# A fused attention and FP4 feed-forward block: one AV copy on ScalarE, division 22 steps behind, and reordered projections, transposes and last divisions

## The reference

```python
def reference(x, Wq, bq, Wk, bk, Wv, bv, Wo, bo, alpha, w_gate, w_up, w_down):   # x: (8, 2048, 1024)
    x = _layernorm(x + attn(x))          # over the last axis, eps 1e-5
    x = _layernorm(x + ffn(x))
    return x

def attn(x):                             # 16 heads of 64
    q, k, v = (x @ W.T + b for each), split into heads
    scores = einsum("bqhd,bkhd->bhqk", q, k) * 64 ** -0.5
    scores = scores * exp(-alpha * abs(i - j))
    out = einsum("bhqk,bkhd->bqhd", softmax(scores), v)
    return out @ Wo.T + bo

def ffn(x):                              # w_gate, w_up: (2816, 1024); w_down: (1024, 2816)
    h = silu(fp4_linear(x, w_gate)) * fp4_linear(x, w_up)
    return fp4_linear(h, w_down)

def fp4_linear(x, w):                    # both quantized and dequantized in blocks of 16
    xq, wq = fp4_quant_dequant(x), fp4_quant_dequant(w)   # scale = max|x| / 6, grid 0 .5 1 1.5 2 3 4 6
    return einsum("bsk,nk->bsn", xq, wq)
```

## Time and profile before

| | |
|---|---|
| median of 3 runs | 1307.09 us (1305.58 to 1398.29) |
| the profiled execution | 1311.45 us |
| its span on the slowest core (core 5) | 1309.9 us |
| spans of the eight cores | 1294.6 to 1309.9 us |
| TensorE busy | 1179.0 us (90%) |
| VectorE busy | 1054.7 us (81%) |
| ScalarE busy | 694.9 us (53%) |
| GpSimd busy | 264.3 us (20%) |
| DMA | 172.58 MB, mean 132 GB/s |

### The profile page before, as it was taken

One profiled execution on the slowest core, in us unless ns is written; L12 is line 12 of the kernel. 1 busy time (PEld: TensorE's weight loads), 2 busy tenths in 40 slices (PEclk: granted clock), 3 DMA queues, 4 the chain that ended last, 5 costly groups with the idle time before them and its releaser, 6 DMA issues.

```text
span 1309.9 us, 19005 instructions; the slowest of 8 cores (1294.6 to 1309.9 us)
## 1 busy us (share of the span) xinstructions
PE 1179.0 (90%) x5856; PEld 459.9 (35%) x5856; DVE 1054.7 (81%) x1360; ACT 694.9 (53%) x809; POOL 264.3 (20%) x444
## 2 busy tenths in 40 slices
PE   3978999999999889898976978899999999999994
PEld 1422233333333223222321323344444444444442
DVE  4686998999999999898986377479888888887873
ACT  2185878788898888888986422212222221222221
POOL 1003132223222222222322144101111101111101
PEclk9998999999999999999997989899999999999998
DMA  9475646465474753766647839973344232324321
GB/s 237 164 154 115 119 106 154 96 133 128 107 142 117 138 136 105 155 152 148 162 120 214 176 121 239 296 213 83 86 105 109 80 90 79 90 79 93 105 65 61
DMA packets 180118, 172.58 MB, mean 132 GB/s; under 512 B 141938, under 2 KB 141938, under 8 KB 178484
## 3 DMA queue, kind: packets, MB, share of 16 engines
q1 hardware_dynamic: 165716, 138.72, 42.4%
q0 software_dynamic: 14304, 32.65, 10.7%
HBM read 111.30 MB, written 34.34 MB: 111 GB/s over the span
## 4 chain that ended last, share of the span: by engine, by line
PE 35%; DVE 29%; DMA 14%; issue 13%; POOL 3%; SPq 2%; ACT 2%; DVEq 1%; POOLq 0%; ACTq 0%
PE ps L1072 15%; PE ps L1154 8%; PE ps L622 4%; DVE qr L240 4%; PE ps L456 3%; DMA recD<-rec_scr 3%; DVE wst L245 3%; DVE Q L488 3%; DMA den_scr<-AV 3%; PE ps L501 2%; DVE wqo L252 2%; PE ps L451 2%; DVE SD L552 2%; DMA xst<-xT 2%; DVE attnT L671 2%
## 5 line engine op out<-in xcount | busy, mean ns | idle before, releaser
L593 ACT ACTIVATE PT<-ps,tab 128x1024 bf16<-128x1024 f32 x384 | 410.5, 1124 | 94.0 <-PE ps L501 93.1
L622 PE MATMUL ps<-PT,V 128*128 128x512 bf16 (+1 forms) x1280 | 307.9, 345 | 7.9 <-DVE AV L646 3.5
L501 PE MATMUL ps<-Q,KT 64*128 64x512 bf16 (+1 forms) x1280 | 205.6, 344 | 45.5 <-DVE SD L552 36.3
L456 PE MATMUL ps<-xTs,wqk 128*128 128x512 bf16 x512 | 146.2, 394 | 37.8 <-ACT xTs L276 17.9
L1072 PE MATMUL ps<-wuT,x1qT 128*128 128x512 bf16 (+1 forms) x768 | 169.4, 364 | 6.4 <-DMA wuT<-wu_scr 4.9
L1072 PE MATMUL ps<-wgT,x1qT 128*128 128x512 bf16 (+1 forms) x768 | 169.5, 364 | 1.7 <-ACT sg L1082 1.3
L1154 PE MATMUL ps<-wdT,hqT 128*128 128x512 bf16 x704 | 154.6, 379 | 0.4 <-DMA hqT<-hq 0.4
L622 PEld LDWEIGHTS ps<-PT,V 128*128 128x128 bf16 x1280 | 92.4, 98 | 168.9 <-issue 150.7
L501 PEld LDWEIGHTS ps<-Q,KT 64*128 64x128 bf16 x1280 | 52.1, 93 | 230.3 <-issue 229.5
L895 ACT ACTIVATE junk<-ring 128x1024 bf16<-128x1024 f32 x15 | 15.9, 1058 | 196.9 <-DVE ring L1165 196.9
L1082 ACT ACTIVATE sg<-ps 128x512 f32<-128x512 f32 (+1 forms) x96 | 50.9, 554 | 119.1 <-PE ps L1072 97.0
(11 more groups left out here) (95 smaller groups left out, 1300.9 us busy)
## 6 DMA issues: line engine op xcount, KB each, us to landing
ring<-x_scr SPq DMA_DIRECT2D x32, 512.0 KB, 4.8
wst<-wg SPq DMA_DIRECT2D x22, 512.0 KB, 4.1
wst<-wu SPq DMA_DIRECT2D x22, 512.0 KB, 4.1
wst<-wd SPq DMA_DIRECT2D x16, 704.0 KB, 5.2
xst<-xT SPq DMA_DIRECT2D x8, 1024.0 KB, 28.5
recD<-rec_scr POOLq DMA_DIRECT2D x64, 128.0 KB, 4.1
out<-ring POOLq DMA_DIRECT2D x15, 512.0 KB, 5.7
wg_scr<-wtr SPq DMA_DIRECT2D x22, 256.0 KB, 4.4
```

The lines of the kernel that those rows point to most:

```text
L456: fn = lambda e, i=i, w=w: e.matmul(out=pt, lhsT=w[:, i, :], rhs=xT[:, c, i, :], start=(i == 0), stop=(i == NCT - 1))
L501: return op(TE, a, lambda e: e.matmul(out=out, lhsT=KT[hp % 2][r0:r0 + 64, kt * 128:(kt + 1) * 128], rhs=QR[u % 3][n][r0:r0 + 64, q0:q1], ...
L593: f = op(AC, k0, lambda e: e.activation(out=PT[ri], in_=src, func=AF.Exp, scale=scl), need)
L622: tok = op(TE, ka, lambda e, h=h, k=k, c0=c0, q0=q0, w=w: e.matmul(out=ps_ab[h][:, q0:q0 + w], lhsT=VV[g][:, k, hp % 4, 8 * h:8 * h + 128] ...
```

## The change

Five edits:

- In units 0 to 3 V's job comes first and K's before Q's. The later units have that order in both kernels.
- Of the two AV copies at the end of a unit, the first head's is made by ScalarE (L644), behind the first exponential of the next unit; VectorE keeps the other. The two denominator rows and cD stand one step later on GpSimd.
- The division stands 22 steps behind instead of 18, and recD's load 6.1 steps behind instead of 2.3. For the last two units, which fall into Wo's part, the keys grow from 38 to 45 and from 33 to 43.
- The loads of x1's first two rows are recorded with `op` instead of `fop` and so do not carry the gate.
- x1's transposes get a key of at least X0 + 58 (tile 0) and X0 + 59 (tile 1).

```diff
@@ -401,13 +401,13 @@
             first_jobs += [("V", 0, t) for t in range(4 * c, 4 * c + 4)]
         jobs = {u: [] for u in range(NU)}
         jobs[0] = [("K", 1, 0), ("K", 1, 1)]
-        jobs[1] = [("Q", 0, 3), ("K", 1, 2)]
-        jobs[2] = [("Q", 1, 0), ("K", 1, 3)]
+        jobs[1] = [("K", 1, 2), ("Q", 0, 3)]
+        jobs[2] = [("K", 1, 3), ("Q", 1, 0)]
         jobs[3] = [("Q", 1, 1)]
         vj = [("V", 1, t) for t in range(NTT)]
         for u in range(NU - 2):
             if u < 16:
-                jobs[u] += vj[:1]
+                jobs[u] = vj[:1] + jobs[u]
                 vj = vj[1:]
             if u < 4:
                 continue
@@ -641,16 +641,16 @@
 
             hp, qc = units[u]
             s = u % 2
-            ev = []
-            for half in range(2):
-                ev.append(dv(ka + 0.1 + 0.01 * half, 0.68, lambda e, half=half: e.tensor_copy(
-                    out=AVs[s][half], in_=ps_ab[half]), [av, norm.get(u - 2)]))
+            ev = [op(AC, max(ka + 0.1, at(u, 15) + 2.15), lambda e: e.activation(
+                out=AVs[s][0], in_=ps_ab[0], func=AF.Identity), [av, norm.get(u - 2)]),
+                dv(ka + 0.1, 0.68, lambda e: e.tensor_copy(
+                    out=AVs[s][1], in_=ps_ab[1]), [av, norm.get(u - 2)])]
             evac[u] = ev
             for half, row in enumerate((64, 56)):
-                t1 = op(PO, ka + 0.5, lambda e, half=half, row=row: e.dma_start(
+                t1 = op(PO, ka + 1.5, lambda e, half=half, row=row: e.dma_start(
                     out=den_d[s:s + 1, half * QC:(half + 1) * QC],
                     in_=AVs[s][half][row:row + 1, :]), ev, sem=d_n1, k=16)
-            t2 = op(PO, ka + 0.6, lambda e: e.dma_start(
+            t2 = op(PO, ka + 1.6, lambda e: e.dma_start(
                 out=cD, in_=den_d[s].rearrange("(p j) -> p j", j=8)), [t1, recip[0]],
                 sem=d_n2, k=16)
             kr = ka + 2.1
@@ -661,11 +661,11 @@
                 out=rec_d[s].rearrange("(p j) -> p j", j=8), in_=cR), [t3], sem=d_n3, k=16)
             rec_st[0] = t4
             for half in range(2):
-                t5 = op(PO, kr + (0.2 if u < NU - 1 else 22.0), lambda e, half=half: e.dma_start(
+                t5 = op(PO, ka + (6.1 if u < NU - 1 else 29.2), lambda e, half=half: e.dma_start(
                     out=recD[64 * half:64 * half + 64, :],
                     in_=rec_d[s:s + 1, half * QC:(half + 1) * QC].broadcast_to([64, QC])),
                     [t4, norm.get(u - 1)], sem=d_n4, k=16)
-            km = ka + {NU - 1: 33.0, NU - 2: 38.0}.get(u, 18.0)
+            km = ka + {NU - 1: 43.0, NU - 2: 45.0}.get(u, 22.0)
             for half in range(2):
                 lo = slice(64 * half, 64 * half + 64)
                 norm[u] = dv(km + 0.1 * half, 0.68, lambda e, half=half, lo=lo: e.tensor_tensor(
@@ -1014,14 +1014,14 @@
             row = ring[1 + s]
             sv, ts = x1_st[tt]
             a = max(t, ts - 2.0, fr_.at + 0.01, sv.at + 0.01)
-            ld = fop(SP, a, lambda e: e.dma_start(out=row, in_=x1_r[tt]),
-                     [fr_, sv], sem=d_rl[s], k=16)
+            ld = (op if tt < 2 else fop)(SP, a, lambda e: e.dma_start(out=row, in_=x1_r[tt]),
+                                         [fr_, sv], sem=d_rl[s], k=16)
             q = tt % 2
             if tt >= 2:
                 force(x1_chain[tt - 2], 7)
 
             def done_(tok, t_):
-                b_ = max([t_ + 0.05] + ([xt_last[tt - 2].at + 0.01] if tt >= 2 else []))
+                b_ = max([t_ + 0.05, X0 + 58.0 + tt] + ([xt_last[tt - 2].at + 0.01] if tt >= 2 else []))
                 x1q_tr[tt] = fop(SP, b_, lambda e: e.dma_start_transpose(
                     out=x1qT[q], in_=x1q[q]), [tok, xt_last.get(tt - 2)],
                     sem=d_xt[q], k=16)
```

## The result

| | before | after |
|---|---|---|
| median of the runs | 1307.09 us | 1273.49 us (4 runs, 1271.53 to 1274.15) |
| ratio to before | | 0.9746, 95% interval 0.9723 to 0.977 |
| the profiled execution, its span | 1311.45, 1309.9 us | 1273.74, 1272.2 us (core 2) |
| spans of the eight cores | 1294.6 to 1309.9 us | 1261.7 to 1272.2 us |

The change takes 2.5% off, 33 us; the forecast was 30. The interval leaves room for 30 to 36 us.

The account below looks back on a forecast made before the run. The prediction took VectorE to bound attention, with TensorE close behind. Its terms, +6 - 9.3 - 10 - 17 + 0 = -30.3 us, taken from the median 1307.09, gave 1277 us, range 1262 to 1299.

Parts of the forecast that it names:

- Part 4: Attention: the division 22 steps behind removes most of VectorE's waits for recD, gaining 17 us, bounds 10 and 23.
- Part 1: Unit 0: V first makes TensorE wait 10.1 us for V's weights, 4.1 come back; costs 6 us, bounds 5 and 10.1.
- Part 2: Units 1 and 2: with Q last, K no longer waits behind Q's copies; gains 9.3 us, bounds 8 and 10.5.
- Part 3: Units 3 to 31: one AV copy on ScalarE relieves VectorE, TensorE bounds next; gains 10 us, bounds 0 and 18.6.
- Part 5: Wo's part and the start of the gate matmuls: no net change, 0 us, bounds -6 and +7.
- (b): Wo's part: the last recD load lands near 776, the division is reached near 769; a wait of some 7 us moves.
- (c): Wo's part: GpSimd's stores still pace tiles 10 to 15; TensorE should be through Wo about 10 us earlier.
- (d): End of Wo's part: x1's first transpose, issued later, lands at 829 to 832 and delays the first gate matmul about 7 us.
- B: Rival: TensorE is not the bound it seems and VectorE's relief counts in full; -44 us, 1263; chance 0.14.
- C: Rival: little comes from the copy and recD's stalls only shrink; -16 us, 1291; chance 0.25.
- D: Rival: x1's late transpose ends last, gate matmuls start 15 us late, nothing given back; -15 us, 1292; chance 0.10.
- E: Rival, slower: ScalarE's copy waits for the last AV matmul, delaying exponentials and TensorE; 1339 at 2 us per unit; chance 0.05.

Follow-up runs that it names:

- V last in unit 0: The changed kernel with V's job last in unit 0 again (K, K, V) and first in units 1 to 15: 1266.08 us, ratio 0.9676.
- short quantization: The changed kernel with the last instruction of each of VectorE's 60 weight chunks on an eighth of its columns or less (output differs): 1258.77 us, ratio 0.9632.
- doubled copy: The changed kernel with ScalarE's AV copy made twice at the same place, the second behind the first: 1281.31 us, ratio 0.9807.

## Where the prediction held and where it failed, part by part

The total agrees: forecast -30 and 1277, measured -33 and 1273.5, inside the range. The way there agrees less, and part of the agreement is luck. By place the forecast was +6 up to the first AV copy, -9.3 in units 1 and 2, -27 in units 3 to 31 and 0 behind them; the table has +7.7, -8.7, -32.1 and -1.4.

The step that failed is in Part 4: "The other four waits sum to 23.2 - 10.1 = 13.1 us ... Gain 13.1 + 5.2". It prices the later division by VectorE's waits for recD alone, and so at nothing in units 3 to 19. The runs show 7.2 us there when it is taken back and 6.9 when it stands alone, from its place in VectorE's order ahead of V's copy, beside 17.5 to 20.3 us in units 20 to 31. Three further steps were off and hid it: the give-back in Part 1 (4.1 us assumed, 1.4 measured), the copy in units 3 to 31 (10 assumed, 3.5 to 5.2 measured), and the 4 to 8 us that the later division costs behind the last AV copy (0 assumed). That the terms simply add held within what the intervals can tell.

**Part 1**, +6: 6.3 on the slowest core, 7.7 by the table, 9.8 by the last AV matmul, and 9 to 10 by taking it back. The mechanism is right. The step that was mis-sized is "what can come back is what VectorE stood idle ... 4.1 us ... since its quantization goes on during the stall": against V last in unit 0 only 11.8 - 10.4 = 1.4 came back. VectorE was busy 21.24 us in the stretch, 22.74 before, so it got no work ahead, and it stood idle 13.4 us, where it had stood idle 4.1. TensorE also went on at its lower clock level for a while (1.44 us for three matmuls instead of 0.81). The landing took 12.5 us from issue instead of 11.6. The wait was 11.8, not 10.1.

**Part 2**, -9.3: -9.8 on the slowest core, -8.7 by the table, -8.8 alone. Right.

**Part 3**, -10 (0 to 18.6): -9 alone, -7 by taking it back. The size was right by luck, since the term was for units 3 to 31, where the copy is worth 3.5 us by the table and 5.2 by the last AV matmul; 3 us (7 where it stands alone) lie behind the last AV copy, which the term did not have. The reading that VectorE is not the only bound held: short quantization does not bring a unit with three jobs under 19.75 to 19.90 us, of which TensorE is busy 19.2 to 19.5. Two things were missed. From unit 21 on ScalarE is as full as TensorE (17.54 of 18.18 us busy; which of the two bounds is not separated), so the copy is worth little there (0.6 to 1.6 us), and in the units at the floor the copy's place costs what the doubled copy showed. The rule of the Trainium skill ("TensorEngine Tiling (Array Packing)", PSUM Bottleneck) would have made the term 18.6; here 3.5 to 5.2 us of it came in units 3 to 31, which fits the floors: splitting the evacuation paid where VectorE was the bound, and hardly elsewhere. The estimate of 570 ns for ScalarE, worked out from the table of the Trainium skill ("VectorE: DVE Perf Modes", section on the TRN2 errata), was nearer in its direction than my row: the copy took 632 against VectorE's 681, and Q's 691, which adds a bias, was not the same work.

**Part 4**, -17 (10 to 23): -21 alone, -20 by taking it back. The failing step, named above, counts only VectorE's waits for recD. What it left out is the place in the order: in units 3 to 19 there was next to no wait for recD (1.2 us once), and the later division is worth 7 us there, because V's copy, and with it K's job, moves ahead. In units 20 to 31 17.5 to 20.3 us came, about the waits with what TensorE waited behind them. Some 4 to 8 us are then given back behind the last AV copy. About 5 of them are TensorE's new wait for wos (before's landed ahead of TensorE, after's 5 us behind it).

**Part 5**, 0 (-6 to +7): -1.4 by the table, -4.5 on the slowest core. (a) Right. (b) Wrong: "A wait has only moved" failed. The load landed 39.5 us behind the last AV copy (744.26 - 704.72; forecast 776 - 738), but VectorE reached the division 42.7 us behind it instead of 31, in part since TensorE had waited 5.25 us for wos and VectorE 3.45 us for a row of x1. The wait for wos, which I had not foreseen, stands in its place. (c) Not borne out: TensorE left Wo's part 85.4 us behind the last AV copy on the profiled core of before and 78.9 on that of after, but the other seven cores of before left it at 75.5 to 79.6, and by the median it is 77.4 before and 79.5 after. The reading of the earlier trace rows was of a core unlike the others. (d) The late transpose was given back as forecast: it cost the first gate matmul 9.3 us on the slowest core, 11 by the table, and none of it reached the down matmuls. The wait for x1's third row is still on the chain that ended last:

```profile
798.91 28.62 DMA ring<-x_scr
```

**Of the signs named** the first AV copy (98), units 1 and 2 (20.7), the last AV copy (704.7 for 708), ScalarE without a wait, the transpose's landing (87.9 us behind the last AV copy for 90) and the down matmuls (128.5 for 133) came. VectorE's waits for recD were 9.8 us in two instead of 5 in one, and the wait of some 7 us for recD in Wo's part did not come. Of the three signs of being wrong one came: by the table the first gate matmul moved by 11.9 us against the last AV copy, over the 10 that I had set (3.0 between the two profiled cores, 85.2 to 88.2).

**The rivals.** B is out: with a floor shown that VectorE does not set, its relief could not count in full. C is out for the stalls (they shrank from 23.2 to 9.8 us with 5 us more) and true for the copy in units 3 to 31 (3 us there; measured 3.5 to 5.2). D's late transpose was given back. E does not turn the sign, but its mechanism exists.

What stays open: whether the place of the last weight chunk is why Wo's part gets 3 to 7 us shorter with the copy on ScalarE, and which engine sets the floor of a late unit. ScalarE's single copy is hardly what sets it: with both copies on VectorE two late units in a row average 18.10 us at the least, against 18.17 in after.

## What to carry to other kernels

Where an instruction waits for a long way through DMA, moving it back can pay twice, as it did here: its own wait goes, and what stood behind it (here the copy that frees the only projection bank) comes sooner, so look at who is next in the queue even where the profile shows no wait. Before the relief of one engine is counted, find each stage's floor by the busy time of the next ones: here 63 us off VectorE bought 15. What was won just ahead of a stage that waits for loads was partly lost in it (4 to 8 us here), and moving the loads about only moved the wait. And look at more than the slowest core: one term here was read from a core that took at least 5.8 us longer in that stage than the other seven.

## What the runs showed of the hardware

- A 2 KB transfer behind a 2 MB load on GpSimd's queue landed with it: the denominators, issued 0.6 us behind wos, which took 20.8 us to land, kept the queue waiting 20.45 us. Large loads on SyncE's queue slowed a small one on GpSimd's too (8.2 us for the 4 KB of cD beside rows of x and wgT, at a DMA share of 0.93).
- Behind an idle time of 11.8 us TensorE stood at its lower clock level (granted clock 0.50 for the next 3.4 us): three 128x512 matmuls took 1.44 and 1.46 us, and 0.81 at granted clock 1.00 some us later.
- ScalarE's fp32 copy of 128x512 from PSUM took 632 ns, VectorE's 681.
